# Attention stage of a fused block: the next pair's normalised rows are written by ScalarE, one tile every six steps

## What is computed

```python
h = _L0_tok_ref(...)                              # mixer: 16 x 128 x 1024
h = concatenate([h, txt], axis=1)                 # 16 x 205 x 1024
h = h + _L0_attn_ref(_layernorm(h), Wqkv, Wo)     # 32 query heads of 32, one key and value head
h = h + _L0_ffn_ref(_layernorm(h), base_W, ...)   # linear layer + routed low-rank experts

def _layernorm(x, axis=-1, eps=1e-05):
    m = jnp.mean(x, axis=axis, keepdims=True)
    v = jnp.var(x, axis=axis, keepdims=True)
    return (x - m) / jnp.sqrt(v + eps)

# attention of one sequence
scores = einsum('bqhd,bkd->bhqk', q, k) * scale + alibi, causal mask
attn   = einsum('bhqk,bkd->bqhd', softmax(scores), v)
```

## Time and profile before

| | |
|---|---|
| runs, median (lowest to highest) | 1653.12 us (1652.87 to 1654.0), 3 runs |
| the profiled execution's own time | 1653.71 us |
| its span, first to last instruction | 1651.9 us |
| mean granted TensorE clock | 0.96 of full speed |
| PE busy | 1476.0 us, 89% of the span |
| DVE busy | 1121.1 us, 68% |
| ACT busy | 735.5 us, 45% |
| POOL busy | 436.4 us, 26% |

### The profile page before, as it was taken

One profiled execution on the slowest core, in us unless ns is written; L12 is line 12 of the kernel. 1 busy time (PEld: TensorE's weight loads), 2 busy tenths in 40 slices (PEclk: granted clock), 3 DMA queues, 4 the chain that ended last, 5 costly groups with the idle time before them and its releaser, 6 DMA issues. The chain is left out here.

```text
span 1651.9 us, 28876 instructions
## 1 busy us (share of the span) xinstructions
PE 1476.0 (89%) x9700; PEld 1316.9 (80%) x9700; DVE 1121.1 (68%) x4158; ACT 735.5 (45%) x2624; POOL 436.4 (26%) x298
## 2 busy tenths in 40 slices
PE   0457299999999999999999789999999999999999
PEld 0456198887888888888887468899998989999897
DVE  7998378888898989898878664444443544444453
ACT  3465158686868778787878431111101011011100
POOL 0233124453544544444445301010010101011010
PEclk9878599999999999999998699999999999999999
DMA  6145366465454646564646231121212111121210
GB/s 210 51 102 111 81 113 116 73 113 88 78 113 72 121 70 124 83 119 70 126 83 138 95 118 54 61 76 38 76 38 76 51 63 67 48 76 38 77 43 33
DMA packets 110521, 139.81 MB, mean 85 GB/s; under 512 B 13156, under 2 KB 96484, under 8 KB 110040
## 3 DMA queue, kind: packets, MB, share of 16 engines
q1 hardware_dynamic: 110408, 138.41, 37.3%
HBM read 62.82 MB, written 40.30 MB: 62 GB/s over the span
## 5 line engine op out<-in xcount | busy, mean ns | idle before, releaser
L720 ACT ACTIVATE P<-P,nmax 128x128 f32<-128x128 f32 (+1 forms) x1024 | 434.6, 426 | 86.2 <-DVE nmax L808 82.4
L782 POOL TENSOR_TENSOR P<-P,rden 128x512 f32<-128x512 f32 (+1 forms) x256 | 330.3, 1312 | 404.3 <-DVE rden L814 404.0
L808 DVE CUSTOM_DVE_ANT_0 P<-sc,mask 128x128 f32<-128x128 f32 (+1 forms) x1024 | 292.2, 323 | 72.3 <-PE sc L615 67.4
L645 PE MATMUL pr<-xT_hi,wq_hi 128*128 128x410 f32 x576 | 242.6, 421 | 0.8 <-DVE xT_lo L824 0.8
L1146 POOL TENSOR_TENSOR h<-h,base_b 128x1024 f32<-128x1024 f32 (+1 forms) x26 | 63.0, 2424 | 640.9 <-DVE xn L1173 640.9
L820 DVE COPY PTR<-pt 128x282 f32<-128x282 f32 x512 | 221.0, 432 | 14.7 <-PE pt L625 13.6
L1057 PE MATMUL b<-w_hi,x2T_hi 128*128 128x390 f32 (+3 forms) x624 | 214.7, 344 | 1.0 <-DVE x2T_lo L1183 1.0
L1057 PE MATMUL b<-w_lo,x2T_hi 128*128 128x390 f32 (+3 forms) x624 | 212.9, 341 | 0.0
L1057 PE MATMUL b<-w_hi,x2T_lo 128*128 128x390 f32 (+3 forms) x624 | 212.6, 341 | 0.0
L645 PE MATMUL pr<-xT_lo,wq_hi 128*128 128x410 f32 x576 | 201.3, 349 | 0.0
L645 PE MATMUL pr<-xT_hi,wq_lo 128*128 128x410 f32 x576 | 200.4, 348 | 0.0
(11 more groups left out here) (174 smaller groups left out, 2913.9 us busy)
## 6 DMA issues: line engine op xcount, KB each, us to landing
Qs<-q_hi SPq DMA_DIRECT2D x128, 205.0 KB, 4.8
Qs<-q_lo SPq DMA_DIRECT2D x64, 205.0 KB, 5.7
att_dram<-att SPq DMA_DIRECT2D x64, 205.0 KB, 2.9
at<-att_dram SPq DMA_DIRECT2D x25, 512.0 KB, 4.8
h<-h_dram SPq DMA_DIRECT2D x25, 512.0 KB, 3.3
out<-h SPq DMA_DIRECT2D x25, 512.0 KB, 2.6
h_dram<-Y SPq DMA_DIRECT2D x64, 128.0 KB, 3.0
ht<-h_dram SPq DMA_DIRECT2D x16, 512.0 KB, 6.1
```

The source lines that it names most:

```text
L645: last = nc.tensor.matmul(out, w[a][:, i, cols], xT[x][:, i, :], start=(i == 0 and m == 0), stop=(i == KC - 1 and m == 2))
L720: last = nc.scalar.activation(P[rows, j % 2, i, cols], P[rows, j % 2, i, cols], ACT.Exp, scale=-1.0, bias=nmax[at], accum_out=den[at])
L782: lastp = nc.gpsimd.tensor_tensor(w, w, r, ALU.mult)
L808: lastv = v.tensor_tensor_reduce(P[0:n, j % 2, i, cols], sc[i % 2][0:n, cols], mask[0:n, m], 1.0, 3.0e38, ALU.add, ALU.min, nmax[0:n, j % ...
```

## The change

The application of the normalisation in the loop moves from VectorE to ScalarE, as scale x row + offset with scale = `rstd` and offset = -mean x `rstd`, both per row. VectorE makes the offsets of all four tiles in one small instruction at step 38, and ScalarE applies them at steps 40, 46, 52 and 58, each time after the exponentials of that step.

```diff
+    offset = sb("ln_offset", [128, 4])
...
-    xn_ready = sem("xn_ready")
+    xn_ready, ln_scaled = sem("xn_ready"), sem("ln_scaled")
+    APPLY_AT, APPLY_EVERY = 40, 6
...
+            def ln_apply(p, s):
+                n = TILES[s][2]
+                act.wait_ge(ln_scaled, p)
+                nc.scalar.activation(ht[0:n, s, :], ht[0:n, s, :], ACT.Identity, scale=rstd[0:n, s:s + 1],
+                                     bias=offset[0:n, s:s + 1]).then_inc(xn_ready, 1)
...
                         if sj is not None:
                             exp_head(*sj, i)
+                        for s in range(4):
+                            if last is False and GH * slot + i == APPLY_AT + APPLY_EVERY * s:
+                                ln_apply(p + 1, s)
...
-        APPLY_AT, APPLY_EVERY = 38, 1
...
+            def ln_offset(link):
+                link.wait()
+                v.scalar_tensor_tensor(out=offset[:], in0=mv[:, :, 0], scalar=-1.0, in1=rstd[:], op0=ALU.mult, op1=ALU.mult).then_inc(ln_scaled, 1)
...
-                            for s in range(4):
-                                if turn == APPLY_AT + APPLY_EVERY * s:
-                                    ln_apply(p + 1, s, link)
+                            if turn == APPLY_AT - 2:
+                                ln_offset(link)
```

## The result

| | before | after |
|---|---|---|
| median of 13 runs, us | 1653.12 (1651.65 to 1654.03) | 1656.64 (1653.18 to 1658.9) |
| ratio of the times | | 1.0020, 95% interval 1.0013 to 1.0027 |
| span of the profiled execution | 1651.9 | 1651.4 |

The account below looks back on a forecast made before the run. TensorE was taken to set the pace, VectorE close behind, with ScalarE nearly full in steps 45 to 54. First pair 2.8 us plus 6 x 0.1 gave 3.4, say 3.5, on 1653.12: 1656.6 us; range 1651.8 to 1659.8.

Parts of the forecast that it names:

- the forecast one: Steps 40 to 59: ScalarE takes VectorE's place as what PE waits for; 1655.0 to 1658.3 us, chance 0.47.
- The tile's cost on ScalarE: Each new ScalarE instruction takes 1.24 us, of which 0.10 overlaps, so 1.15 us a tile; bounds 0.95 and 1.25.
- The rival of the copy's price: On ScalarE, a tile costs only what a Copy does, its per-row operands nothing: -0.8 us, 1652.3; chance 0.20.
- The first pair: While the first pair runs, ScalarE has no slack, so PE's transposes of step 59 start 2.8 us late.
- The six later pairs: From the second pair on, PE's gain at step 43 is given back by step 59: 0.1 us later each.
- The walk: ScalarE's queue followed from step 40 at 495.07: the q_hi of step 56 starts at 512.8 to 512.9, not 511.87.
- The sum: Whole run: 2.8 us for the first pair plus 6 x 0.1 gives 3.4, say 3.5 us slower.
- The fourth tile: Step 58: forecast covered, at no cost to PE; the rival, uncovered, adds 0.4 us x 7, 1659.4; chance 0.22.
- The gain of step 43: PE's transposes of step 43 no longer wait for VectorE's copy behind a tile: 0.97 us a pair gained.
- The gain stays: Rival: ScalarE's tiles are hidden whole, PE keeps 0.97 us in each of six pairs: 1647.3 us; chance 0.06.
- the distance of two pairs: Sign in the profile after: from one pair to the next takes 89.5 to 89.7 us.
- three points that would have made me wrong: Pair distance falling 0.5 us or more; PE's loss at step 61 or later; first pair not about 3 us longer.

Follow-up runs that it names:

- the second comparison: The changed kernel measured once more, unaltered, against the kernel before: median 1655.85 us against 1653.03.
- no per-row operands: Changed kernel with a Copy with constant scale in place of ScalarE's Identity with scale and offset per row: median 1653.84 us against 1653.03 before.
- 1.00 alone: Kernel before without VectorE's four tiles for pairs 1 to 7, nothing added to ScalarE: median 1648.11 us against 1653.01; relief 1.00 us a pair.
- the early tiles: Changed kernel with ScalarE's tiles of later pairs at steps 37, 38, 39 and 58, the first pair's on VectorE: median 1647.59 us against 1653.01 before.
- the first run of the early tiles: Changed kernel with ScalarE's tiles at steps 37, 38, 39 and 58 in every pair, the first included: 1651.39 us, one run, against 1652.53 before.
- the changed kernel's third trace: The changed kernel run a third time, unaltered: 1655.70 us, one run, against 1653.51 for the kernel before.

## Why the prediction was right, and where it was off

The time, 1656.6, is the measured 1656.64, and the cause is the forecast one. That the last digits meet is luck: one term was off by 1.0 us, the interval of the measurement is wider than that, and the second comparison gives 2.8 us for the same change.

- *The tile's cost on ScalarE*, 1.24 us with 0.10 of overlap: measured 1.230, and 1.14 to the next start. The rival of the copy's price is out (no per-row operands). The Trainium skill's rule (ScalarE: Activation LUTs, What ACT_TABLE_LOAD costs), 93 ns for each pointer operand, agrees with this trace for two: 92 ns each. No tile brought a table load: the traces before and after both have 11 of them, and one, of 1.28 us, in the attention stage.
- *The first pair*, 2.8: measured 2.79 in three traces. The sum was right, its path only in part. I had followed the two q_lo, with waits of about 2 us at steps 49 and 57; they wait 1.74 and 0.93. I had not seen that VectorE's reciprocal of step 45 is the first to wait (1.94 us), nor counted that PE wins 0.97 us at step 43 in this pair as well. PE loses 1.56 at step 47, 1.52 at 51 and 0.73 at 58, less 0.97 at 43 and 0.10 at 42. Since all of these hang on one queue that doesn't idle, its length decides the sum.
- *The six later pairs*, +0.1 each: measured -0.06. This is the term that was mis-sized, by 0.16 us, in all 1.0 us. The walk put the q_hi of step 56 at 512.8 to 512.9, and it starts at 512.61: sixteen heads at 0.835 and three tiles at 1.14 instead of 0.84 and 1.15 make 0.11 of this; the walk began 0.03 us late, and the rest is rounding up. Behind step 51 PE still had 0.8 of its 1.0 us, where I had put half.
- *The sum*, 3.5: the stages show 2.4 in the attention (2.8 - 0.4). The measured 3.5 has an interval of 2.1 to 4.5 and the second comparison, 2.8, one of 1.3 to 4.3, so the missing 1.1 us is not resolved; nothing in the traces gives it a place.
- *The fourth tile* is covered: shown by leaving it out, and the cover ends with less than one tile more. VectorE's wait at the reciprocal of step 61, put at 0.4, is 0.39.
- *The gain of step 43*, 0.97: 1.03 in the trace, 1.00 alone. *The gain stays* would have been the case at another place, as the early tiles show, at 1647.6, where the rival had put it (1647.3). I had tied it to the cost of a tile ("below about 0.8 us"); the place decides as well.
- My forecast that the distance of two pairs is 89.5 to 89.7 us was missed by 0.06 to 0.10; none of the three points that would have made me wrong came about.

## What to carry to other kernels

An engine's busy share over a stage doesn't say where it has room: ScalarE had 20 us free in a pair, and some 2 us in the 16 steps in which it got 3.4 us of new work. Walk the queue from the last point at which the engine waited to the next result that others need, in each kind of iteration, the first one by itself. Here, once the queue had no gap left, what was taken from it came out at its end whole (0.55 us of three tiles, in both kinds of pairs). A few steps earlier the same instructions were all but free in the later pairs (88.56 us against 88.50 without them), but not in the first pair (58.37 against 56.34), where the gap ahead of them was partly a wait for their own input.

## What the runs showed of the hardware

- An ACTIVATE of 1024 columns takes 1.046 us as Copy with a constant scale and 1.230 as Identity with a scale and an offset per row, for 77 rows as for 128 (1.226 to 1.258 over all 28). The next instruction starts 1.14 us after it.
- The granted TensorE clock can fall from 1.00 to 0.50, of the two levels 2.4 and 1.2 GHz the lower, for about 3 us in the middle of the attention stage, in one execution and not in the next of the same kernel. With ScalarE's tiles in the first pair it fell there in four traces of nine; PE had waited 1.20 us at step 48 ahead of it in the first run of the early tiles, and 1.33 in the changed kernel's third trace. The trace after has a wait of 1.32 us in the same place and no drop. The four traces without these tiles in the first pair have none. It cost 0.97 us in one kernel and nothing in three runs, where PE had a wait behind it anyway. Which executions have it, and how much of the wider spread of the changed kernel's times it makes, stays open.
